# Two layers of a graph network on one core: counting the edges of each bucket in one run or in two

## The chip, the core and the metric

The kernel runs on one core of a Trainium2 chip. The metric is the device time of one launch in microseconds. Five engines work side by side, each with an instruction queue of its own: TensorE (PE), VectorE (DVE), ScalarE (ACT), GpSimd (POOL) and SyncE (SP), whose queue issues most of the DMAs. They meet through semaphores: an instruction adds to one, and a queue waits until it has reached a value.

## What is computed

1250 nodes with 512 features, 21250 edges (20000 random ones and a loop at each node), sorted by destination. A three-layer network takes at each node the mean of its neighbours' features; an edge network with a segment sum and two layer norms follow. Cut to what the change touches:

```python
deg = jax.ops.segment_sum(jnp.ones_like(dst, dtype=x.dtype), dst, num_segments=n)
inv_deg = (1.0 / jnp.clip(deg, 1.0))[:, None]
for l in range(n_layers):
    neigh = jax.ops.segment_sum(h[src], dst, num_segments=n) * inv_deg
    h = h @ Ws_self[l] + neigh @ Ws_neigh[l] + bs[l]
    if l != n_layers - 1:
        h = jax.nn.relu(h)
```

The kernel writes the segment sum as a product with the matrix A of counts: A[d, s] is the number of edges from s to d, and deg is the sum of a row.

## The kernel before

**Buckets and tiles.** The nodes are cut into NB = 10 buckets of NPB = 125 by destination. The edges lie as 125 rows of EC = 170 columns in SBUF. Each edge gets a slot, so that the edges of a bucket fill whole tiles of 128; there are TILES = 176. With this data a bucket has 17 tiles (one has 18), 171 in all, and the last five are empty.

**Phase A** (`phase_a`, up to 412.86 us in the profile) has two strands.
- *Sorting.* VectorE works out the slots (`rows_of`, L389 on: first for 34 columns, then for 136) and the tables of tiles (L407 to L417: first tile of each bucket, bucket of each tile). POOL then scatters the edges' records (8 numbers) to the table `records` in HBM by indirect DMAs, a column each: `stage` (L319) copies 17 columns and issues 17 DMAs, ten times. When all 170 have landed, SP loads the table as `recs` (L296).
- *Products.* Beside it TensorE folds weight matrices, multiplies the mesh features, and does the first layer's dense products for ten blocks of nodes (L662 on), with VectorE and ScalarE splitting numbers into a high and a low part (`w_hi`, `w_lo`; `u_hi`, `u_lo`). The products are done at 256 us.

*Counting* comes last. For each tile VectorE makes two one-hot matrices (`one_hot`, L494), from the sources (128 x 1280, L497) and from the destinations (128 x 128, L498). There are GROUP = 4 buffers, so VectorE is at most four tiles ahead. TensorE multiplies them (`count`, L684) in ten 128 x 128 matmuls (L689) that add to PSUM banks 0 to 2, and one (L692) that adds the degrees to bank 3. The banks are never cleared: after a bucket's last tile ScalarE copies them out (L575, L577) to `adj[:, c]` and `degree[:, c]`, so that each copy is a running total, and phase B takes neighbours' difference.

*Gates.* A tile must not add to a bank before the copy of the bucket before is out. TensorE's loop waits for `gate[b][u]`, counted up once a tile for each of three banks. SP opens those of even tiles, and POOL those of odd ones, both with `open_gates`:

```python
with engine.Fori(0, TILES // 2) as i:
    bucket1 = engine.value_load(k["tile_bucket1"][0:1, ds(2 * i + u, 1)], min_val=1, max_val=NB)
    for b in range(3):
        engine.wait_ge(copied_out[b], bucket1)
        engine.sem_inc(gate[b][u], 1)
```

In the trace L225 is this loop (address, counter, branch), L226 the load of a register from the table, with two register operations, and L229 the three increments.

**Phase B** (`phase_b`) begins behind a barrier of all engines. `own_counts(n)` (L848) takes the difference of two running totals on VectorE (L851). ScalarE and VectorE split it (`convert` L972, `rest` L864), TensorE sums over the neighbours (`add_up`, L1042 and L1043), and `mix` (L871) divides by the degree. At the start VectorE does own_counts(9), the degrees, own_counts(8) and `many_i` (L936), which TensorE waits for before it starts. Ten blocks follow, then the dense product of the next layer. SP loads that layer's weights to `w0` and `w1` at once. The edge network and the last layer norms come behind; they fill most of the time and aren't touched.

## Time and profile before

| | us |
|---|---|
| median of three runs | 2359.06 (2358.61 to 2361.78) |
| the profiled execution | 2361.97 |
| its span | 2360.3 |
| TensorE busy | 2217.3, 94% of the span |
| VectorE busy | 1473.0, 62% |
| ScalarE busy | 1217.3, 52% |
| GpSimd busy | 1129.5, 48% |
| mean granted clock of TensorE | 0.979 of full |

Busy time is that of compute instructions (and of POOL's making of indirect DMAs). Register, branch and semaphore instructions aren't in it, so a queue that only counts semaphores shows as idle. "idle before, releaser" says how long an engine stood still before an instruction, and what ended it. The stages that the change touches lie between 0 and 475 us.

### The profile page before, as it was taken

Reading aid. Unit: us, or ns where it says so; the run is one execution under the profiler, and the core shown is the slowest. Engines: PE = TensorE matmul, PEld = TensorE weight load, DVE = VectorE, ACT = ScalarE, POOL = GpSimd, SP = SyncE. Lnnn points to the kernel's source line nnn. Section 1 sums busy time; section 2 is a strip of 40 time slices with the busy share of each in tenths; the row PEclk is TensorE's granted clock in tenths of the full one; section 3 lists DMA queues with packets and bytes.
Section 4 is the critical chain, followed back from the end, with each engine's and each line's share of the span. In section 5 each row is a group of like instructions: output and inputs, shape, how many; then the busy total and the mean of one; then the engine's idle time right before and its main releaser. Section 6 shows DMA issues by size and latency. Waiting matters only on the chain. (4 is left out here: it accounts for less than half of the span.)

```text
span 2360.3 us, 44804 instructions
## 1 busy us (share of the span) xinstructions
PE 2217.3 (94%) x13056; PEld 1889.3 (80%) x13060; DVE 1473.0 (62%) x3261; ACT 1217.3 (52%) x2255; POOL 1129.5 (48%) x1666
## 2 busy tenths in 40 slices
PE   2999399999999999999999999999999999999798
PEld 2436298778777998989989899898988989889686
DVE  7012299534384667767676767766776677666566
ACT  0122111324234767666767677676766676667421
POOL 6777700000012556555555555565656565555323
PEclk9999699999999999999999999999999999999899
DMA  7223100101126433323333333332333333333031
GB/s 204 79 61 74 20 0 0 36 5 37 40 86 186 121 63 62 65 60 64 63 65 62 62 62 62 62 66 59 62 67 62 62 62 66 60 61 67 19 92 44
DMA packets 79034, 150.48 MB, mean 64 GB/s; under 512 B 17048, under 2 KB 18148, under 8 KB 78977
## 3 DMA queue, kind: packets, MB, share of 16 engines
q0 software_dynamic: 44864, 93.18, 20.7%
q1 hardware_dynamic: 34113, 56.57, 7.6%
q8 instruction: 33, 0.54, 0.1%
q14 instruction: 24, 0.20, 0.0%
HBM read 129.17 MB, written 20.23 MB: 63 GB/s over the span
## 5 line engine op out<-in xcount | busy, mean ns | idle before, releaser
L1453 ACT ACTIVATE b_bank<-c_bias 128x512 f32<-128x512 f32 x528 | 316.1, 599 | 15.1 <-PE b_bank L1556 5.2
L1256 POOL DMA_INDIRECT c_from_src<-s_dst_table,c_at_nodes x173 | 297.2, 1718 | 31.1 <-issue 31.1
L1633 PE MATMUL b_bank<-c_m_hi,c_pt_hi 128*128 128x512 f32 x704 | 293.2, 417 | 0.0
L1390 DVE CUSTOM_DVE_ANT_0 b_bank<-b_bank,c_p,k_floor 128x512 f32<-128x512 f32 x176 | 132.4, 752 | 255.1 <-PE b_bank L1578 254.3
L1634 PE MATMUL b_bank<-c_m_lo,c_pt_hi 128*128 128x512 f32 x704 | 276.2, 392 | 0.0
L1243 POOL DMA_INDIRECT c_from_src<-s_mesh_table,c_at_nodes x176 | 202.4, 1150 | 153.8 <-POOL c_at_nodes L1239 143.6
L1635 PE MATMUL b_bank<-c_m_hi,c_pt_lo 128*128 128x512 f32 x704 | 275.6, 391 | 0.0
L1262 POOL TENSOR_TENSOR c_dev<-c_var,k_half 128x1 f32<-128x1 f32 x176 | 99.3, 564 | 312.6 <-DVE c_var L1372 312.6
L1517 ACT ACTIVATE c_h<-c_from_src 128x512 f32<-128x512 f32 x176 | 111.3, 632 | 265.0 <-DVE c_from_src L1411 265.0
L330 POOL DMA_INDIRECT s_records<-a_stage_rec,a_stage_row x170 | 206.0, 1212 | 57.4 <-issue 53.1
L1576 PE MATMUL b_bank<-c_m_hi,c_ht_hi 128*128 128x384 f32 x704 | 223.0, 317 | 4.9 <-DVE c_ht_lo L1377 4.6
L1576 PE MATMUL b_bank<-c_m_hi,c_pt_hi 128*128 128x384 f32 x704 | 224.7, 319 | 0.0
L1578 PE MATMUL b_bank<-c_m_hi,c_ht_lo 128*128 128x384 f32 x704 | 218.8, 311 | 0.0
L1577 PE MATMUL b_bank<-c_m_lo,c_ht_hi 128*128 128x384 f32 x704 | 217.9, 309 | 0.0
L1578 PE MATMUL b_bank<-c_m_hi,c_pt_lo 128*128 128x384 f32 x704 | 217.1, 308 | 0.0
L1577 PE MATMUL b_bank<-c_m_lo,c_pt_hi 128*128 128x384 f32 x704 | 216.9, 308 | 0.0
L842 POOL TENSOR_TENSOR b_dev<-b_dev,k_half 125x1 f32<-125x1 f32 x10 | 5.9, 603 | 397.8 <-DVE b_dev L889 397.8
L1406 DVE SCALAR_TENSOR_TENSOR c_rp_lo<-c_p,c_dev,c_rp_hi 128x512 fp32r<-128x512 f32 x176 | 132.2, 751 | 78.2 <-ACT c_rp_hi L1513 74.2
L1635 PEld LDWEIGHTS b_bank<-c_m_hi,c_pt_lo 128*128 128x128 f32 x704 | 132.5, 188 | 32.0
L1513 ACT ACTIVATE c_rp_hi<-c_p,c_dev 128x512 fp32r<-128x512 f32 x176 | 127.6, 725 | 55.9 <-POOL c_dev L1278 55.8
L1449 ACT ACTIVATE c_p<-b_bank 128x512 f32<-128x512 f32 x176 | 105.7, 600 | 91.2 <-PE b_bank L1553 90.7
L689 PE MATMUL a_bank<-a_hot_dst,a_hot_src 128*128 128x128 bf16 x1760 | 111.0, 221 | 42.7 <-DVE a_hot_dst L498 37.5
(307 smaller groups left out, 5927.7 us busy)
## 6 DMA issues: line engine op xcount, KB each, us to landing
k_w<-in_L_gnn_Ws_self_dram SPq DMA_DIRECT2D x3, 1024.0 KB, 9.0
k_w<-in_L_gnn_Ws_neigh_dram SPq DMA_DIRECT2D x3, 1024.0 KB, 11.5
c_from_src<-s_mesh_table,c_at_nodes POOLq DMA_INDIRECT x176, 3.5
c_from_src<-s_dst_table,c_at_nodes POOLq DMA_INDIRECT x173, 4.8
s_records<-a_stage_rec,a_stage_row POOLq DMA_INDIRECT x170, 2.6
a_mesh<-in_L_gnn_mesh_nfeat_dram SPq DMA_DIRECT2D x10, 224.0 KB
k_h<-in_x_dram SPq DMA_DIRECT2D x1, 2240.0 KB
s_mesh_table<-a_mesh_out SPq DMA_DIRECT2D x10, 224.0 KB
```

The source lines that it names most:

```text
L330: pool.indirect_dma_start(scratch["records"], bass.IndirectOffsetOnAxis(ap=stage_row[u][:, c:c + 1], axis=0), stage_rec[u][:, c, :], None) ...
L1243: pool.indirect_dma_start(from_src[u][:], None, scratch["mesh_table"], bass.IndirectOffsetOnAxis(ap=at_nodes[u][:, 0:1], axis=0)).then_inc ...
L1256: pool.indirect_dma_start(from_src[u][:], None, scratch["dst_head" if head else "dst_table"], bass.IndirectOffsetOnAxis(ap=at_nodes[u][:, ...
L1390: dve.tensor_tensor_reduce(var1_bank[:], var1_bank[:], p[u % 2][:], 1.0 / D, k["floor"][:, 0:1], ALU.mult, ALU.add, var[u][:, 0:1]).then_i ...
L1406: dve.scalar_tensor_tensor(out=rp_lo[u][:], in0=p[u % 2][:], scalar=dev[u][:, 0:1], in1=rp_hi[u][:].bitcast(F32), op0=ALU.mult, op1=ALU.su ...
L1453: act.activation(bank[:], bias[:, m, :], ACT.Copy).then_inc(bank_set, 1)
L1576: pe.matmul(to, left[0][:, c, :], high, start=False, stop=False, skip_group_check=True)
L1577: pe.matmul(to, left[0][:, c, :], low, start=False, stop=False, skip_group_check=True)
L1578: last = pe.matmul(to, left[1][:, c, :], high, start=False, stop=(c == KC - 1), skip_group_check=True)
L1633: pe.matmul(edge_bank[:], left[0], m_hi[1][:, c, :], start=False, stop=False, skip_group_check=True)
L1634: pe.matmul(edge_bank[:], left[0], m_lo[1][:, c, :], start=False, stop=False, skip_group_check=True)
L1635: last = pe.matmul(edge_bank[:], left[1], m_hi[1][:, c, :], start=False, stop=(c == KC - 1), skip_group_check=True)
```

## The change

- The first COLS1 = 136 columns (8 of 10 stagings) are scattered to `records`, the last 34 to a second table, `records2`. VectorE works out totals at column 136 and at 170, and a second offset for the last columns. An edge's slot stays within its bucket, with the first 136 columns' edges in front.
- Tiles that the first 136 columns fill (12 or 13 a bucket, 129 in all with this data) are counted first, bucket by bucket, and the remaining 47 in a second run. So the banks are copied out EVENTS = 20 times. `order`, `place` and `event1` are built on VectorE; TensorE turns the source and destination fields by transposes and a product with `place` into the order of counting (`turn_columns`, `place_fields`), and VectorE copies them to `fields`.
- SP loads the first table as soon as 136 columns are scattered, and the second between the two halves of its gate loop. VectorE adds both at tile 100, and the fields from tile 108 on are made anew.
- POOL scatters to the end and then makes the two `w_lo` of the next layer, instead of VectorE. Its gate loop is gone; SP opens the gates of all tiles, two in an iteration.
- ScalarE writes the second run's copies to `adj_more`, partly over `w0` and `w1`, and the tenth copy a second time to `adj_mid`. Phase B adds the runs (`merge`) before it takes differences, adds two degrees, and loads the next weights only when all ten counts are done.
- The tile tables are built behind the centring of the weights, not ahead of it.

```diff
+COLS1 = 8 * SCAT
+EVENTS = 2 * NB
...
+SECOND = 25
...
-    def open_gates(engine, u):
-        engine.wait_ge(tables_ok, 1)
-        with engine.Fori(0, TILES // 2) as i:
-            bucket1 = engine.value_load(k["tile_bucket1"][0:1, ds(2 * i + u, 1)], min_val=1, max_val=NB)
-            for b in range(3):
-                engine.wait_ge(copied_out[b], bucket1)
-                engine.sem_inc(gate[b][u], 1)
+    def open_gates(engine, first, end):
+        with engine.Fori(first, end) as i:
+            for u in range(2):
+                before1 = engine.value_load(event1[0:1, ds(2 * i + u, 1)], min_val=1, max_val=EVENTS)
+                for b in range(3):
+                    engine.wait_ge(copied_out[b], before1)
+                    engine.sem_inc(gate[b][u], 1)
...
+        for u in range(2):
+            sp.wait_ge(scattered[u], 16 * COLS1 // 2)
+        sp.dma_start(recs[:], scratch["records"].rearrange("(p t) f -> p t f", p=P)).then_inc(recs_in, 16)
         sp.wait_ge(self_ok, NB)
         sp.dma_start(bias0[:], rows(t["L0_gnn_bs"][1]).broadcast_to([P, D])).then_inc(bias_next, 16)
-        for u in range(2):
-            sp.wait_ge(scattered[u], 16 * EC // 2)
-        sp.dma_start(recs[:], scratch["records"].rearrange("(p t) f -> p t f", p=P)).then_inc(recs_in, 16)
         for u in range(2):
             sp.wait_ge(job_out[u], 16 * (NJ // 2) + 16 * ((len(vectors) + 1 - u) // 2))
             sp.wait_ge(mesh_stored[u], MOVED * NB // 2)
         sp.wait_ge(bias_next, 16)
-        open_gates(sp, 0)
+        sp.wait_ge(tables_ok, 1)
+        open_gates(sp, 0, TILES // 4)
+        for u in range(2):
+            sp.wait_ge(scattered2[u], 16 * (EC - COLS1) // 2)
+        sp.dma_start(k["part2"][:], scratch["records2"].rearrange("(p t) f -> p t f", p=P)).then_inc(part2_in, 16)
+        open_gates(sp, TILES // 4, TILES // 2)
...
+        pool.memset(k["part2"][:], 0.0).then_inc(pool_const, 1)
...
-            stage(u, 0, True)
+            stage(u, 0, True, scratch["records"], scattered)
         pool.wait_ge(rows_ok, 2)
-        with pool.Fori(1, EC // (2 * SCAT)) as j:
+        with pool.Fori(1, COLS1 // (2 * SCAT)) as j:
             for u in range(2):
-                stage(u, j, False)
-        open_gates(pool, 1)
+                stage(u, j, False, scratch["records"], scattered)
+        pool.wait_ge(rows_ok, 3)
+        pool.wait_ge(pads2_out, 16)
+        for u in range(2):
+            stage(u, COLS1 // (2 * SCAT), True, scratch["records2"], scattered2)
+        for i in range(2):
+            pool.wait_ge(w_next_hi, i + 1)
+            pool.tensor_tensor(w_lo[i][:], w[i][:], w_hi[i][:].bitcast(F32), ALU.subtract).then_inc(w_next_lo, 1)
...
-        rows_of(slice(0, 2 * SCAT))
-        rows_of(slice(2 * SCAT, EC))
...
+        rows_of(slice(0, 2 * SCAT), offset)
+        rows_of(slice(2 * SCAT, COLS1), offset)
+        dve.tensor_copy(counts1[:], bank[1][:, 0:NB])
+        chain.after(dve.tensor_tensor(offset2[:], bank[0][0:EP, NB:2 * NB], totals[:, 0:NB], ALU.subtract))
+        chain.after(dve.tensor_tensor(offset2[:], offset2[:], bank[0][0:EP, 0:NB], ALU.subtract))
+        chain.after(dve.tensor_tensor(offset2[:], offset2[:], counts1[0:EP, :], ALU.add))
+        chain.after(dve.scalar_tensor_tensor(out=offset2[:], in0=starts[0:EP, :], scalar=float(P), in1=offset2[:],
+                                             op0=ALU.mult, op1=ALU.add))
+        rows_of(slice(COLS1, EC), offset2)
...
+        for c in range(EVENTS - 1):
+            dve.tensor_scalar(step_by[:], tile_no[:, 0:TILES], event_at[:, c:c + 1], jump[:, c:c + 1], ALU.is_ge, ALU.mult)
+            chain.after(dve.scalar_tensor_tensor(out=event[:], in0=tile_no[:, 0:TILES], scalar=event_at[:, c:c + 1],
+                                                 in1=event[:], op0=ALU.is_ge, op1=ALU.add))
+            chain.after(dve.tensor_tensor(order[:], order[:], step_by[:], ALU.add))
+        for c in range(2):
+            dve.tensor_scalar(place[c][:], order[:], part_no[:, c:c + 1], None, ALU.is_equal)
+        dve.tensor_copy(event1[:], event[:]).then_inc(tables_ok, 1)
...
+        dve.wait_ge(part2_in, 16)
+        dve.tensor_tensor(recs[:], recs[:], k["part2"][:], ALU.add).then_inc(recs_ok, 1)
+        for u in range(GROUP):
+            one_hot(GROUP * SECOND + u, u)
+        copy_columns(2)
+        for u in range(GROUP):
+            one_hot(GROUP * (SECOND + 1) + u, u)
+        copy_fields(2, GROUP * (SECOND + 2))
...
+        for c in range(EVENTS):
+            done = act.value_load(event_end[0:1, c:c + 1], min_val=1, max_val=TILES + 1) if c < EVENTS - 1 else TILES + 1
+            if c == NB:
+                act.wait_ge(w_next_lo, 2)
+            to = k["adj"][:, c, :] if c < NB else k[f"adj_more{c - NB}"][:]
             for b in range(3):
                 lo, hi = b * 512, min((b + 1) * 512, NB * P)
                 act.wait_ge(count_mm[b], done)
-                last = act.activation(k["adj"][:, c, lo:hi], bank[b][:, 0:hi - lo], ACT.Copy)
+                last = act.activation(to[:, lo:hi], bank[b][:, 0:hi - lo], ACT.Copy)
+                if c == NB - 1:
+                    last = act.activation(k["adj_mid"][:, lo:hi], bank[b][:, 0:hi - lo], ACT.Copy)
                 if b == 2:
-                    last = act.activation(k["degree"][:, c:c + 1], bank[3][:, 0:1], ACT.Copy)
+                    last = act.activation(k["degree_at"][:, c:c + 1], bank[3][:, 0:1], ACT.Copy)
...
+        for u in range(2 * GROUP):
+            count(GROUP * SECOND + u, u % GROUP)
+            if u == 0:
+                pe.wait_ge(recs_ok, 1)
+                turn_columns()
+            if u == GROUP + 1:
+                place_fields(2)
...
+                sp.wait_ge(counts_ok, NB)
...
+            if n:
+                merge(n - 1)
             own = k["adj"][0:NPB, n, :]
-            dve.tensor_tensor(own, own, k["adj"][0:NPB, n - 1, :], ALU.subtract).then_inc(counts_ok, 1)
+            dve.wait_ge(merged, NB - max(n - 1, 0))
+            dve.tensor_tensor(own, own, k["adj"][0:NPB, n - 1, :] if n else k["adj_mid"][0:NPB, :],
+                              ALU.subtract).then_inc(counts_ok, 1)
+        def merge(n):
+            both = k["adj"][0:NPB, n, :]
+            dve.tensor_tensor(both, both, k[f"adj_more{n}"][0:NPB, :], ALU.add).then_inc(merged, 1)
...
+        merge(NB - 1)
         own_counts(NB - 1)
-        dve.tensor_copy(degree[:, 0:1], k["degree"][:, 0:1])
-        dve.tensor_tensor(degree[:, 1:], k["degree"][:, 1:], k["degree"][:, 0:NB - 1], ALU.subtract).then_inc(degree_ok, 1)
+        dve.tensor_copy(degree_runs[:, 0:1], k["degree_at"][:, 0:1])
+        dve.tensor_tensor(degree_runs[:, 1:], k["degree_at"][:, 1:], k["degree_at"][:, 0:EVENTS - 1],
+                          ALU.subtract).then_inc(runs_ok, 1)
         dve.memset(ones[:], 1.0)
+        dve.wait_ge(runs_ok, 1)
+        dve.tensor_tensor(degree[:], degree_runs[:, 0:NB], degree_runs[:, NB:], ALU.add).then_inc(degree_ok, 1)
```

**Where instructions move.** SP's queue at the end of phase A, before: the load of the records (L296), and a loop with one register load, one tile.

```order
L290 DMA k_w<-in_L_gnn_Ws_neigh_dram 128x4x512
L292 DMA b_bias_53<-in_L_gnn_bs_dram 128x512
L296 DMA k_recs<-s_records 128x1408
L225 UNCONDITIONAL_BRANCH
L225 ISA
L226 TENSOR_LOAD k_tile_bucket
L226 ISA x2
L225 REGISTER_ALU
L225 COMPARE_AND_BRANCH
```

And now, from the same load of weights on:

```order
L315 DMA k_w<-in_L_gnn_Ws_neigh_dram 128x4x512
L318 DMA k_recs<-s_records 128x1408
L320 DMA b_bias_53<-in_L_gnn_bs_dram 128x512
L247 UNCONDITIONAL_BRANCH
L247 ISA
L249 TENSOR_LOAD a_event_106
L249 ISA x3
L249 TENSOR_LOAD a_event_106
L249 ISA x2
L247 REGISTER_ALU
L247 COMPARE_AND_BRANCH
L329 DMA a_part_62<-s_records 128x1408
```

The records' load stands ahead of bias0's; the loop has two register loads, one counter and one branch, and stands a second time behind the second table's load. POOL's queue has no such loop any more.

VectorE's queue at the start of phase B, before:

```order
L851 TENSOR_TENSOR k_adj<-k_adj 125x1280
L925 COPY b_degree<-k_degree 128x1
L926 TENSOR_TENSOR b_degree<-k_degree 128x9
L927 MEMSET b_ones 128x2
L929 TENSOR_REDUCE b_most<-b_degree 128x1
L930 TENSOR_SCALAR b_inv_degree<-b_degree 125x10
L932 TENSOR_SCALAR b_many<-b_most 128x1
L933 TENSOR_SCALAR b_many<-b_most 128x1
L851 TENSOR_TENSOR k_adj<-k_adj 125x1280
L936 CAST b_many_i<-b_bank 1x2
```

And now:

```order
L1001 TENSOR_TENSOR k_adj<-k_adj,ab_adj_more_72 125x1280
L1001 TENSOR_TENSOR k_adj<-k_adj,ab_adj_more_71 125x1280
L995 TENSOR_TENSOR k_adj<-k_adj 125x1280
L1076 COPY ab_degree_runs<-ab_degree_at 128x1
L1077 TENSOR_TENSOR ab_degree_runs<-ab_degree_at 128x19
L1079 MEMSET b_ones 128x2
L1081 TENSOR_TENSOR k_degree<-ab_degree_runs 128x10
...
L1001 TENSOR_TENSOR k_adj<-k_adj,ab_adj_more_70 125x1280
L995 TENSOR_TENSOR k_adj<-k_adj 125x1280
L1090 CAST b_many_i<-b_bank 1x2
```

Two merges (L1001) stand ahead of the first own_counts (L995), a third ahead of the second, and one addition of degrees (L1081) ahead of the maximum; all of them come before `many_i`.

## Rows read from the trace of the kernel before

**Rows 1.** Windows: stage, us, busy us of each engine (instructions), granted clock, DMA share.

```profile
256.20:294.31 38.11, 0.81 (x3) 0.32 (x4) 5.28 (x4) 3.48 (x2) 26.45 (x21) 0.53 0.14 29
294.31:412.86 118.55, 111.07 (x1936) 106.00 (x1936) 112.46 (x352) 14.26 (x40) 0.00 (x0) 0.98 0.00 0
412.86:417.93 5.07, 0.19 (x3) 0.10 (x3) 3.04 (x12) 2.20 (x3) 0.00 (x0) 0.79 0.33 93
```

**Rows 2.** Timeline, 232 to 295: start, us, engine, line, operation, idle before it.

```profile
232.10 0.21 POOL L324 COPY a_stage_row<-a_row_i 125x17 int32 x1
...
249.88 0.69 DVE L482 TENSOR_TENSOR k_h<-a_bank,b_bias 125x512 f32<-125x512 f32 x1 [4.12 <-PE a_bank L66]
...
256.20 0.35 SPq L292 DMA_DIRECT2D b_bias<-in_L_gnn_bs_dram  x1
257.91 4.67 DVE L488 TENSOR_TENSOR b_w_lo<-k_w,b_w_hi 128x2048 fp32r<-128x2048 f32 x2 [1.10 <-ACT b_w_hi L567]
...
290.21 0.34 SPq L296 DMA_DIRECT2D k_recs<-s_records  x1
294.31 0.55 DVE L497 TENSOR_SCALAR a_hot_src<-a_src_grid,k_recs 128x1280 bf16<-128x1280 int16 x1 [31.73 <-DMA k_recs<-s_records]
```

**Rows 3.** Timeline of one border between two buckets, 396.9 to 398.7.

```profile
396.94 0.17 PE L692 MATMUL a_bank<-a_ones,a_hot_dst 128*128 128x2 bf16 x1
396.97 0.72 PE L689 MATMUL a_bank<-a_hot_dst,a_hot_src 128*128 128x128 bf16 x10
...
397.39 1.36 ACT L575 ACTIVATE k_adj<-a_bank 128x512 int16<-128x512 f32 x3 [9.93 <-PE a_bank L689]
397.53 0.17 PE L692 MATMUL a_bank<-a_ones,a_hot_dst 128*128 128x2 bf16 x1
398.63 0.19 ACT L577 ACTIVATE k_degree<-a_bank 128x1 f32<-128x1 f32 x1
```

**Rows 4.** Lines L226, L225 and L229, SP's queue: duration ns, first and last start.

```profile
L226 SPq TENSOR_LOAD <-k_tile_bucket x8: 267/270/273, 308.9 to 316.7; - x8
...
L225 SPq ALU_OP  x2: 32/32/33, 295.5 to 296.6; - x2
L225 SPq FUSED_REGOPS  x2: 59/59/59, 295.8 to 296.9; - x2
...
L225 SPq MOVE  x1: 29/29/29, 290.8 to 290.8; - x1
...
L229 SPq EVENT_SEMAPHORE  x24: 17/17/17, 291.8 to 299.9; - x24
```

**Rows 5.** Waits of SP's queue, 240 to 410: for whom, us, times, longest.

```profile
SPq L229 <- ACT k_adj L575: 18.9, 18, 5.7
SPq L229 <- ACT k_degree L577: 2.8, 9, 0.3
```

**Rows 6.** Timeline of VectorE, 12 to 30.

```profile
13.56 1.74 DVE L392 SCALAR_TENSOR_TENSOR a_scan<-a_scan,a_offset,a_mask 125x34 f32<-125x34 f32 x10
23.75 0.35 DVE L407 TENSOR_SCALAR a_tile_bucket<-a_tile_no,a_starts 128x177 f32<-128x177 f32 x1
28.94 2.28 DVE L422 TENSOR_REDUCE a_mean<-a_w 128x4 f32<-128x2048 f32 x1
```

**Rows 7.** DMA issues, 255 to 262: KB, us from issue to landing.

```profile
b_bias<-in_L_gnn_bs_dram SPq DMA_DIRECT2D x1, 256.0 KB, 3.1
```

**Rows 8.** Timeline of the second phase's start.

```profile
414.83 0.82 DVE L851 TENSOR_TENSOR k_adj<-k_adj 125x1280 int16<-125x1280 int16 x1 [3.94 <-PEq L2001]
417.93 0.79 PE L1042 MATMUL b_bank<-b_u_hi,b_a_hi 125*128 125x512 f32 x1 [1.45 <-DVE b_many_i L936]
```

**Rows 9.** Timeline of the first layer's sums in steady state.

```profile
436.68 1.49 DVE L864 TENSOR_TENSOR b_a_lo<-k_adj,b_a_hi 125x1280 fp32r<-125x1280 int16 x1 [1.13 <-ACT b_a_hi L972]
```

**Rows 10.** Timeline of TensorE at the counting's start.

```profile
297.29 1.23 PE L689 MATMUL a_bank<-a_hot_dst,a_hot_src 128*128 128x128 bf16 x10
...
298.38 1.23 PE L689 MATMUL a_bank<-a_hot_dst,a_hot_src 128*128 128x128 bf16 x10
```

More of the change, by code:

```diff
@@ L154, in phase_a @@
     hot_dst = [hot(f"a_hot_dst{i}", [P, P], BF16) for i in range(GROUP)]
-    totals, offset = sb("totals", [EP, NB]), sb("offset", [EP, NB])
+    order, event, step_by = (hot(f"a_{n}", [P, TILES]) for n in ("order", "event", "step_by"))
+    place = [hot(f"a_place{i}", [P, TILES]) for i in range(2)]
+    columns_t, fields = hot("a_columns_t", [P, 4, P]), hot("a_fields", [P, 2, TILES])
+    event1 = hot("a_event1", [P, TILES], I32)
+    totals, offset, offset2 = sb("totals", [EP, 2 * NB]), sb("offset", [EP, NB]), sb("offset2", [EP, NB])
+    counts1, full, rest, full_ends, rest_ends = (
+        sb(n, [P, NB]) for n in ("counts1", "full", "rest", "full_ends", "rest_ends"))
+    full_i, event_end = sb("full_i", [P, NB], I32), sb("event_end", [P, EVENTS], I32)
+    event_at, jump = sb("event_at", [P, EVENTS]), sb("jump", [P, EVENTS])
+    part_no = sb("part_no", [P, 2])
     slot_i, slot_lo, slot_hi = (sb(n, [EP, EC], I32) for n in ("slot_i", "slot_lo", "slot_hi"))
@@ L387, in _, with rows_of @@
                                              op0=ALU.mult, op1=ALU.add))
-        def rows_of(part):
+        def rows_of(part, offset):
             for c in range(NB):
@@ L445, in _ @@
             last.then_inc(gains_ok, 1)
+        dve.wait_ge(pool_const, 7)
+        chain.after(dve.tensor_scalar(tile_bucket[:], tile_no[:], starts[:, 1:2], None, ALU.is_ge))
+        for c in range(2, NB):
+            chain.after(dve.scalar_tensor_tensor(out=tile_bucket[:], in0=tile_no[:], scalar=starts[:, c:c + 1], in1=tile_bucket[:],
+                                                 op0=ALU.is_ge, op1=ALU.add))
+        chain.after(dve.memset(tile_bucket[:, TILES:], float(NB)))
+        chain.after(dve.tensor_tensor(tile_step[:], tile_bucket[:, 1:], tile_bucket[:, :TILES], ALU.subtract))
@@ new lines, in _ @@
+        chain.after(dve.scalar_tensor_tensor(out=tile_flag[:], in0=tile_bucket[:, :TILES], scalar=1.0, in1=tile_step[:],
+                                             op0=ALU.add, op1=ALU.mult))
+        dve.tensor_copy(k["tile_last"][:], tile_flag[:])
+        dve.tensor_scalar(k["tile_bucket1"][:], tile_bucket[:, :TILES], 1.0, None, ALU.add)
+        dve.tensor_copy(k["bucket_end"][:], ends[:])
+        chain.after(dve.tensor_copy(full_i[:], counts1[:]))
+        chain.after(dve.tensor_scalar(full_i[:], full_i[:], 7, None, ALU.logical_shift_right))
@@ new lines, in _ @@
+        chain.after(dve.tensor_copy(full[:], full_i[:]))
+        chain.after(dve.tensor_tensor(rest[:], tiles_f[:], full[:], ALU.subtract))
+        dve.tensor_tensor_scan(out=full_ends[:], data0=full[:], data1=k["zeros"][:, 0:NB], initial=0.0,
+                               op0=ALU.add, op1=ALU.add)
+        chain.after(dve.tensor_tensor_scan(out=rest_ends[:], data0=rest[:], data1=k["zeros"][:, 0:NB], initial=0.0,
+                                           op0=ALU.add, op1=ALU.add))
+        dve.tensor_copy(event_at[:, 0:NB], full_ends[:])
@@ new lines, in _ @@
+        chain.after(dve.tensor_scalar(event_at[:, NB:], rest_ends[:], full_ends[:, NB - 1:NB], None, ALU.add))
+        dve.tensor_scalar(event_end[:], event_at[:], 1.0, None, ALU.add)
+        dve.tensor_copy(jump[:, 0:NB - 1], rest[:, 0:NB - 1])
+        dve.tensor_copy(jump[:, NB:EVENTS - 1], full[:, 1:NB])
+        chain.after(dve.tensor_tensor(jump[:, NB - 1:NB], full[:, 0:1], full_ends[:, NB - 1:NB], ALU.subtract))
+        chain.after(dve.tensor_tensor(jump[:, NB - 1:NB], jump[:, NB - 1:NB], rest_ends[:, NB - 2:NB - 1], ALU.subtract))
@@ new lines, in _ @@
+        dve.tensor_copy(order[:], tile_no[:, 0:TILES])
+        chain.after(dve.memset(event[:], 1.0))
+        for c in range(EVENTS - 1):
[3 more added lines that the diff above has]
+            chain.after(dve.tensor_tensor(order[:], order[:], step_by[:], ALU.add))
@@ L583, in _ @@
         pe.wait_ge(dve_const, 4)
[L584 removed]
+        pe.wait_ge(pool_const, 7)
         pe.wait_ge(totals_ok, 1)
[L586 to L587 removed]
+        pe.matmul(bank[0][0:EP, 0:2 * NB], before[0:EP, 0:EP], totals[:], start=True, stop=True)
+        pe.matmul(bank[1][:, 0:2 * NB], ones[0:EP, :], totals[:], start=True, stop=True).then_inc(totals_mm, 1)
         pe.wait_ge(centred, 3)
```

143 lines of the change are left out of this document (90 added, 53 removed).

## The prediction

> **What bounds the kernel now.** I read the windows by stage first. Between 256.20 and 294.31 us TensorE does 0.81 us of work; the counting stage runs from there to 412.86, 118.55 us; then 5.07 us pass with almost nothing on TensorE [rows 1]. TensorE is busy 94% of the whole span (the table above) and everything behind the counting is chained to it, so a microsecond gained or lost here moves the end by about as much. The timeline of the gap shows its cause: VectorE starts the first one-hot at 294.31 after 31.73 us of waiting for the records, whose load SP issued at 290.21, when the last scatter had landed [rows 2]. That gap is what the change goes for.
>
> Then the counting stage itself. VectorE is busy 112.46 of its 118.55 us with 352 operations, two for each of 176 tiles, 0.64 us a tile [rows 1]: it sets the pace. TensorE could go a little faster: the closing matmuls (L692) of two neighbouring tiles start 0.59 us apart at the full clock [rows 3]. But TensorE also waits for gates, and these are made by two instruction queues, SP for even tiles, POOL for odd ones. So I read SP's queue, which the busy shares leave out. In a stretch with nothing to wait for, eight register loads of L226 go from 308.9 to 316.7, which is 7.8/7 = 1.11 us for one gate iteration, one tile [rows 4]. 88 of them are 98 us. The waits of SP in this stage come to 18.9 + 2.8 us [rows 5]. Together 120 us, the length of the stage: SP has had only some 20% of its time to spare, with half of the tiles.
>
> **The change part by part, in the profiled execution's time (2361.97, span 2360.3; the median of the runs is 2359.06, 2.9 lower, and I carry the difference over).**
>
> Start. The tile tables (23.75 to 28.94 us on VectorE [rows 6]) move behind the centring, into time in which VectorE is idle; a third call of rows_of with ten 34-column operations (1.74 us [rows 6]) and its tail, 3.3 in all by the like steps, and four small ones on offset2 (0.9) come before it, while the middle call gets shorter by 1.0. Net 5.2 - 3.3 - 0.9 + 1.0 = 2.0; with the two added small operations I take 1.6 us earlier for TensorE's chain up to 256. Ends: 0 (the weights' load decides) and 2.0. The memset, the zero table's store, the event tables (19 rounds of three short operations, about 20 us) and columns_t lie in VectorE's and SP's idle time; I cost them at nothing. Without that cover the tables would cost those 20 us.
>
> Records. POOL stages column 136 and its sixteen followers at 232.10, so the first 136 have landed near 235; the load takes 294.31 - 290.21 = 4.1 us, so 239. The product loop's last step asks for it after the ninth step's matmuls, near 249 [rows 2]: ten us of slack. The first one-hot could start near 257. **But the gates can't open then**: SP loads bias0 at 256.20 as before, it lands in 3.1 us [rows 2, 7], and SP enters its loop at 259.3 - 1.6 = 257.7.
>
> Gates. This is the term that decides. POOL's loop is gone, since POOL scatters; SP now runs all 176 tiles, two in an iteration. What the pair saves is one add, one branch and the jump: from ALU_OP at 296.6 to the next FUSED_REGOPS at 296.9 [rows 4], which I take as 0.24. So a pair costs 2 x 1.115 - 0.24 = 1.99 us, 1.0 a tile, against 0.64 that VectorE needs. 88 pairs: 175.1, plus 0.3 for entering (MOVE at 290.8 to the first gate at 291.8 [rows 4]). **SP becomes the pace.** VectorE's additions in the stage (the sum of both tables about 1.7 us, copies of columns and fields about 1.2) hide in the 0.36 us a tile that it now waits; TensorE's eight transposes and four-matmul groups do too.
>
> Events. Banks are copied out 20 times instead of 10, with 19 borders to pass instead of 9. At a border SP now stands in the wait itself. From the rows of one border [rows 3]: the bucket's last tile starts at 396.97, ScalarE at 397.39, 0.42 later; degree's copy ends at 398.63 + 0.19 = 398.82, 1.43 after ScalarE's start. The third gate of the next tile then opens 0.42 + 1.43 + 0.1 - 0.09 = 1.86 us after the third gate of the last one, against 1.0 without a border: 0.86 each, 19 x 0.86 = 16.3. The tenth copy is made twice (adj_mid), 1.4 more. SP's load of the second table between its two loops costs 0.7; it is issued near 350, 60 us after the scatter's end, and has some 8 us until VectorE, at most four tiles ahead, needs it: 4.1 are enough.
>
> End of counting: 257.7 + 175.1 + 0.3 + 16.3 + 1.4 + 0.7 = 451.5 for the last gate, and 0.42 + 1.43 - 0.09 to the last copy, 453.3. Before it is 412.86: **40.4 us later**.
>
> w_lo. Two operations of 4.67 us together [rows 2] go from VectorE to POOL behind the scatter, at 290; ScalarE asks for them at the eleventh copy, near 400. Hidden, and would be at ten times the price.
>
> Second phase. Ahead of the first sum VectorE has three merges more, each like L851's 0.82, and a degree addition with its wait. Two merges stand before own_counts(9), one before own_counts(8), all in front of many_i, for which TensorE waits before it starts at 417.93 [rows 8]: 3 x 0.82 + 0.3 = 2.8 us. The merges inside the loop lie in a wait: the L864 in the steady state had waited 1.13 us for ScalarE [rows 9], a merge takes 0.82. The weights' load now waits for the tenth count, still a whole layer ahead of its use. Ends: 0.8 (one merge) and 5.
>
> Sum: 40.4 + 2.8 = 43.2. **2359.06 + 43.2 = 2402 us**, 1.8% slower; the profile would say 2405. A measurement of this kernel tells 0.2%, 4.7 us, from no change.
>
> Bounds. For a gated tile, 0.875 (the loop's 0.24 saved on each) and 1.115 (on none) are the ends: 154 and 196 us, a total of 2381 to 2423. I take 1.0, since the loads, register operations and six semaphore steps are the same and only their loop end is shared. For a border the ends are 0.6, if half of the copies ran beside the next load, and 1.4, the whole copy: 2397 to 2412.
>
> **A rule weighed.** Tiles at 297.29 and 298.38 show the low level of the clock: 1.09 us a tile against 0.59 at the full one [rows 3, 10]; they follow the long gap, whose granted clock is 0.53 [rows 1]. With gates at 1.0 us TensorE works 0.6 of the time. If it fell to the low level there, 1.09 would replace 1.0. The Trainium skill (TensorE: Matmul & The Clock Gate, Part 1) says that the low level comes after an idle window and names a kernel whose short pauses between groups of matmuls made the clock swing between 1.2 and 2.4 GHz. By its first statement nothing is added to my sum; by the second up to the price of rival 2. No stretch of this trace has such a rhythm.
>
> **Rivals.**
> 1. *SP keeps up, faster.* If a tile's gates in the longer body cost under 0.64, VectorE stays the pace. Then counting starts at 256.2 instead of 294.31 and takes 118.55 + 2.9 for VectorE's additions, 10 x 0.6 for borders (VectorE's idle 6.1 us in the stage lie at nine borders and the cold start [rows 1]), 1.4 for adj_mid: 385.1, 27.8 earlier, less 2.8 behind: 2334 us. For it: the gap in [rows 1] is real and all of the other terms are small. Against it: [rows 4]; the body would have to run 1.8 times as fast. The deciding point is 1.0 - 43.2/176 = 0.75 us a tile: below it the new kernel wins. Chance 8%.
> 2. *The low clock holds in the gated stage.* A tile takes 1.09, 176 x 0.09 = 16 more at most, and a border's 0.42 grows to some 0.7, 5 more; a fully busy TensorE regains the clock, so about half of that: 2412. Chance 12%.
> 3. *The gate loop binds only in part*, because SP's lead or the borders hide one another: 10 us less, 2392. This lies in the forecast's own range; chance 10%. That the change doesn't do what it says would show as a records wait of VectorE before its first one-hot; the ten us of slack in [rows 2] speak against it, and I give it nothing of its own.
>
> **How the numbers follow.** Forecast 68%, rival 3 10%, rival 2 12%, rival 1 8%, within 0.2% 2% (several errors of one sign). Range: 2387 to 2420, which leaves out rival 1 and the corners of both bounds. Faster 0.08, same 0.02, slower 0.90.
>
> **What the profile would show.** Right: the gap at 256 gone, the first one-hot near 257, the first count near 259; VectorE's L-lines of one_hot waiting for TensorE in nearly every tile; TensorE waiting for SPq some hundred times; SP's register loads 0.9 and 1.1 apart by turns; counting about 194 us long; own counts near 455. Wrong: SP with long waits for ScalarE and loads faster than 0.75 apart, or counting ended before 400.

## The result, and the profile after

The change takes 2412.74 us (median of four runs, 2408.44 to 2413.62) beside 2360.42 for the kernel before on the same chip: a ratio of 1.0222 [1.021, 1.0235], 2.2% slower. Of the four executions of the kernel before that stand beside it one took 3005.05 us; the other three have the median 2359.06, and the change is 53.7 above it. I had forecast 2402, slower, within 2387 to 2420. The profiled execution took 2408.44 us (span 2406.7), where I had expected the profile to say 2405.

Windows of the changed kernel, as in [rows 1]: the start, the counting before, in and behind a stall, and the start of the second phase.

```profile
256.40:260.90 4.50, 1.86 (x9) 0.92 (x9) 4.01 (x10) 3.50 (x2) 3.82 (x5) 1.00 0.22 62
260.90:287.40 26.50, 19.66 (x275) 17.00 (x275) 21.50 (x45) 1.43 (x4) 21.91 (x17) 0.94 0.08 3
287.40:296.20 8.80, 2.19 (x20) 1.89 (x21) 8.80 (x9) 1.43 (x4) 6.42 (x2) 0.56 0.00 0
296.20:461.00 164.80, 117.27 (x1656) 96.63 (x1653) 105.88 (x298) 25.87 (x72) 0.00 (x0) 0.98 0.01 5
461.00:466.50 5.50, 0.00 (x0) 0.00 (x0) 3.09 (x12) 1.78 (x5) 0.00 (x0) 0.63 0.00 0
```

The 38 us gap is gone, and the counting behind it fills 201 us in place of 118.55. In the last long window neither engine is full: TensorE 117 and VectorE 106 of 164.80 us, where VectorE had 112.46 of 118.55 [rows 1]. Something that is in no column sets the pace. The waits between 255 and 460 us name it (for whom, us, times, longest):

```profile
DVE a_hot_src L584 <- PE a_bank L820: 54.0, 123, 2.0
PE a_bank L817 <- SPq L252: 52.2, 156, 2.5
...
PE a_bank L817 <- DVE a_hot_dst L585: 9.9, 5, 7.5
```

VectorE waits for TensorE, and TensorE 156 times for an increment of SP's queue (L252, the gates). SP's own waits for the copies (230 to 470) are short but for one of 7.6 us, which is the stall below; so its queue is busy and not held up:

```profile
SPq L252 <- ACT k_adj L676: 12.9, 14, 7.6
SPq L252 <- ACT ab_degree_at L680: 6.1, 19, 0.6
SPq L252 <- ACT ab_adj_more L676: 5.8, 14, 0.6
```

The register loads of the gate loop, from 262 to 270 us (duration ns, first and last start), correspond to [rows 4]:

```profile
L249 SPq TENSOR_LOAD <-a_event x8: 262/270/315, 262.3 to 269.1; - x8
```

Eight loads are 6.8 us apart, 0.97 a tile; followed one by one they stand 0.9 and 1.1 us apart by turns, up to the last at 459.5.

The timeline holds one thing that I had not foreseen. When the last scatter's issue ends, near 285, GpSimd does the two w_lo, and VectorE stands inside a single one-hot until both are done (start, us, as in [rows 2]):

```profile
283.54 0.23 DVE L585 TENSOR_SCALAR a_hot_dst<-a_dst_grid,a_fields 128x128 bf16<-128x128 int16 x1
...
284.16 9.72 DVE L585 TENSOR_SCALAR a_hot_dst<-a_dst_grid,a_fields 128x128 bf16<-128x128 int16 x1
...
284.85 8.96 POOL L382 TENSOR_TENSOR b_w_lo<-k_w,b_w_hi 128x2048 fp32r<-128x2048 f32 x2
...
293.93 1.25 PE L817 MATMUL a_bank<-a_hot_dst,a_hot_src 128*128 128x128 bf16 x10 [7.46 <-DVE a_hot_dst L585]
...
294.58 1.36 ACT L676 ACTIVATE k_adj<-a_bank 128x512 int16<-128x512 f32 x3 [19.80 <-PE a_bank L817]
```

The same operation takes 0.23 us a moment earlier. The one that stands has the earlier start of the two, 284.16 against 284.85. The last counting, the merges and the first sum correspond to [rows 8]:

```profile
461.86 0.19 ACT L680 ACTIVATE ab_degree_at<-a_bank 128x1 f32<-128x1 f32 x1
463.32 1.56 DVE L1001 TENSOR_TENSOR k_adj<-k_adj,ab_adj_more 125x1280 int16<-125x1280 int16 x2 [5.47 <-PEq L2155]
...
469.08 0.78 PE L1196 MATMUL b_bank<-b_u_hi,b_a_hi 125*128 125x512 f32 x1 [2.31 <-DVE b_many_i L1090]
```

The last copy ends at 462.05 against 412.86, 49.2 later (forecast 40.4); the first sum starts 51.15 later than at 417.93.

### The profile page after: what moved, and what is told of

The parts are those of the page before. It is cut to its first block and busy times, and to the rows that moved or that the text cites. A ratio compares the mean times of both kernels' runs of the same rounds, so it can differ in the third digit from the quotient of the medians.

```text
span 2406.7 us, 44790 instructions
## 1 busy us (share of the span) xinstructions
PE 2244.7 (93%) x13080; PEld 1897.9 (79%) x13084; DVE 1537.0 (64%) x3375; ACT 1234.0 (51%) x2298; POOL 1123.4 (47%) x1669
## 5 line engine op out<-in xcount | busy, mean ns | idle before, releaser
L1397 POOL DMA_INDIRECT c_from_src<-s_mesh_table,c_at_nodes x176 | 196.8, 1118 | 154.0 <-POOL c_at_nodes L1393 144.7
L817 PE MATMUL a_bank<-a_hot_dst,a_hot_src 128*128 128x128 bf16 x1760 | 136.3, 224 | 63.4 <-SPq L252 52.4
L817 PEld LDWEIGHTS a_bank<-a_hot_dst,a_hot_src 128*128 128x128 bf16 x1760 | 104.0, 100 | 86.7 <-SPq L252 41.4
```

What stands on the lines that cost most here:

```text
L817: last = pe.matmul(bank[b][:, (s % 4) * P:(s % 4 + 1) * P], hot_src[u][:, s * P:(s + 1) * P], hot_dst[u][:], start=False, stop=False, skip ...
L1397: pool.indirect_dma_start(from_src[u][:], None, scratch["mesh_table"], bass.IndirectOffsetOnAxis(ap=at_nodes[u][:, 0:1], axis=0)).then_inc ...
```

## The experiments

Theory A: SP's queue, with a register load and three waits a tile, is the pace. Theory B: VectorE and GpSimd shut each other out while GpSimd does w_lo. The rivals: the twenty copies and VectorE's additions make the loss; the low clock does; the stall is a wait for something else.

All results in one table; the last copy's start and the first sum are read in the timeline of each profiled execution, the median stands beside a kernel before at 2359.1 to 2360.4.

| kernel | last degree copy | first sum | median us | ratio to before |
|---|---|---|---|---|
| before | 412.67 | 417.93 | 2359.06 | 1 |
| the change | 461.86 | 469.08 | 2412.74 | 1.0222 [1.021, 1.0235] |
| e0_again | 458.34 | 465.58 | 2410.09 | 1.0219 [1.0201, 1.0236] |
| e1_wlo_vector | 456.10 | 463.33 | 2406.34 | 1.0196 [1.0179, 1.0213] |
| e2_two_queues | 412.36 | 420.66 | 2368.93 | 1.0038 [1.0026, 1.0051] |
| e3_before_sp | 471.77 | 476.28 | 2418.42 | 1.0248 [1.023, 1.0265] |
| e4_runs | 405.93 | 413.16 | 2354.21 | 0.9979 [0.9969, 0.9988] |
| e5_runs_vector | 398.81 | 406.04 | 2348.16 | 0.9952 [0.9935, 0.9969] |
| e6_runs_late_bias | 398.78 | 406.01 | 2350.34 | 0.9956 [0.994, 0.9973] |
| e7_two_queues_vector | 409.19 | 417.52 | 2362.23 | 1.0015 [1.0005, 1.0024] |
| e8_before_runs | 407.32 | 411.82 | 2355.72 | 0.998 [0.997, 0.9989] |
| e9_wlo_twice | 415.45 | 422.68 | 2363.42 | 1.0021 [1.0011, 1.003] |
| e10_wlo_pieces | 409.81 | 417.04 | 2353.40 | 0.9974 [0.9963, 0.9985] |
| e11_best_again | 399.75 | 406.98 | 2346.28 | 0.9946 [0.9933, 0.996] |

### The change once more, and w_lo back on VectorE

e0_again is the change, unedited. Expected:

> The changed kernel once more, beside the same runs of before as the next three. Every theory: 2.1 to 2.3% slower, 2408 to 2414 us, counting ended (last copy out of PSUM) near 462 us. The profiled execution of the change was 2408.4 and the three others 2412 to 2414; the theory that this spread is TensorE's clock in the last phase expects that the granted clock behind 2280 us goes with it, and that the stages up to there agree within 1 us.

The median is within the expected range. But this second profiled execution ends its counting 3.5 us earlier than the first, and not within 1 us of it. The expectation on the clock holds: behind the first sum it takes 1941.5 us, with a granted clock of 0.88 over its last 156 us, where the first took 1937.6 with 0.92. In its timeline the stall is there, but TensorE waits at another place:

```profile
285.07 10.11 DVE L584 TENSOR_SCALAR a_hot_src<-a_src_grid,a_fields 128x1280 bf16<-128x1280 int16 x1
...
295.40 1.25 PE L817 MATMUL a_bank<-a_hot_dst,a_hot_src 128*128 128x128 bf16 x10 [7.00 <-DVE a_hot_dst L585]
```

SP goes on opening gates while VectorE stands, until the next border between buckets. In the first execution that border came in the middle of the stall, and two neighbouring loads there were 9.11 us apart in place of 1.64: 7.5 lost. Here it came later, 5.66 in place of 1.64: 4.0 lost.

e1_wlo_vector:

```diff
-        for i in range(2):
-            pool.wait_ge(w_next_hi, i + 1)
-            pool.tensor_tensor(w_lo[i][:], w[i][:], w_hi[i][:].bitcast(F32), ALU.subtract).then_inc(w_next_lo, 1)
...
         copy_fields(1, 0)
+        for i in range(2):
+            dve.wait_ge(w_next_hi, i + 1)
+            dve.tensor_tensor(w_lo[i][:], w[i][:], w_hi[i][:].bitcast(F32), ALU.subtract).then_inc(w_next_lo, 1)
```

> The two w_lo go back from GpSimd to VectorE, ahead of the first one-hot, and nothing else. Theory 'VectorE and GpSimd shut each other out': in the profile of the change one L585 takes 9.72 us while GpSimd makes the w_lo (8.96 us from 284.85), TensorE waits 7.46 us; this goes, and the 4.7 us on VectorE at 258 hide in the 0.36 us that it waits per tile: 8 to 9 us less than e0. Rival 'the stall is a late gate or record, and w_lo only stands beside it': the stall stays, 0 to 3 us more than e0.

Measured 3.75 us less than e0_again, under half of what I expected. No operation of VectorE near 285 is longer than 3 us any more, and TensorE's waits for VectorE are 7.8 us, the longest (5.0) at the start. I had priced the whole stall; but SP's pace hides the part of it up to the next border, and 4.0 is what e0_again had left to win. SP's loads at both borders stand 1.64 apart here, and from its first load to its last it takes 192.8 us in place of 196.5.

### Two queues for the gates

e2_two_queues keeps everything of the change, and lets GpSimd open the odd tiles' gates once SP has opened the first 36 tiles:

```diff
-        open_gates(sp, 0, TILES // 4)
+        open_gates(sp, 0, 18)
+        sp.sem_inc(handed, 1)
+        open_half(sp, 0, 18, TILES // 4)
...
+        pool.wait_ge(handed, 1)
+        open_half(pool, 1, 18, TILES // 2)
```

> SP opens all gates of the first 36 tiles, and from there on SP those of even and GpSimd those of odd tiles, as before the change; w_lo stays on GpSimd. Theory 'SP's gate loop is the pace': up to tile 36 as in e0 (near 306 us), then 140 tiles at 0.64 plus 17 borders at 0.65, the tenth copy 1.4 and VectorE's additions 3: last copy near 412 instead of 462, the kernel at 2360 to 2364, no change against before. Rival 'the twenty copies, the merging of tables and the longer queue of VectorE are the price': less than 10 us better than e0.

46 us of counting come back, with all twenty copies, VectorE's additions and GpSimd's w_lo still in place: those rivals are out as the main cause. The last copy is where it was expected; the median is 5 us above the range that I gave and 9 above before's, while the profiled execution was the fastest of the six. TensorE's waits from 255 to 470 us:

```profile
DVE a_hot_src L596 <- PE a_bank L832: 17.1, 31, 1.6
PE a_bank L829 <- SPq L252: 9.0, 23, 2.5
PE a_bank L829 <- DVE a_hot_dst L597: 8.2, 3, 7.0
```

e3_before_sp puts the suspected cost alone into the kernel before: no second run, no additions, only SP for all gates.

```diff
         with engine.Fori(0, TILES // 2) as i:
+            for u in range(2):
...
-        open_gates(pool, 1)
```

> The kernel before, with its gates opened by SP alone, two tiles in an iteration; nothing else of the change. Theory 'SP's gate loop is the pace': 88 pairs at 1.99 us and 9 borders at 0.86 from 290.8 on, the last copy at 476 instead of 413 us, 63 us slower than before (2.6%). Rival 'two queues' worth of work fits in one, since the waits are shared': slower by less than 10 us.

The last copy comes 59.1 us later and the kernel is 58.5 slower (63 expected). Its first one-hot came 3.0 us earlier than in the profile of before, so the stage itself grew by 62.1 us. Its waits in the same stretch, and eight register loads from 300 to 308 us:

```profile
DVE a_hot_src L497 <- PE a_bank L692: 51.3, 156, 0.8
PE a_bank L689 <- SPq L230: 45.3, 155, 0.7
```

```profile
L227 SPq TENSOR_LOAD <-k_tile_bucket x8: 262/264/273, 300.2 to 308.0; - x8
```

It is the pattern of the change, in a kernel that has nothing else of it. Theory A is shown from both sides, and for most of the loss: e1_wlo_vector, the change without the stall, is still 46.5 us slower than before.

### A cheaper loop on one queue

e4_runs asks whether SP as such is slow, or only this loop. The copies are waited for once a run of tiles, and the loop over its tiles only counts up; TensorE waits for one gate a bank (`gate[b][0]`, n + 1).

```diff
-        with engine.Fori(first, end) as i:
-            for u in range(2):
-                before1 = engine.value_load(event1[0:1, ds(2 * i + u, 1)], min_val=1, max_val=EVENTS)
+        for c in range(first, end):
+            at = engine.value_load(event_end[0:1, c - 1:c], min_val=1, max_val=TILES) if c else 1
+            stop = engine.value_load(event_end[0:1, c:c + 1], min_val=1, max_val=TILES + 1) if c < EVENTS - 1 else TILES + 1
+            for b in range(3):
+                engine.wait_ge(copied_out[b], c + 1)
+                engine.sem_inc(gate[b][0], 1)
+            with engine.Fori(at + 1, stop):
                 for b in range(3):
-                    engine.wait_ge(copied_out[b], before1)
-                    engine.sem_inc(gate[b][u], 1)
+                    engine.sem_inc(gate[b][0], 1)
```

> The change with another gate loop, still SP alone: each of the 20 runs of tiles between two copies waits for the copies once, and the loop over its tiles holds only three increments, no register load of a table and no wait. Counts on TensorE, copies, borders and w_lo on GpSimd are those of the change. Theory A (SP's loop with its load, waits and increments is the pace at 1.0 us a tile): SP now takes under 0.5 us a tile, VectorE at 0.64 is the pace again; stage 112.6 for 176 tiles, 19 borders x 0.65, 1.4 for adj_mid, 3.3 for the additions of VectorE, and now the whole 8.8 us in which VectorE and GpSimd shut each other out: last degree copy near 398.5, against 458 to 462 in the change; kernel near 2347, faster than before. TensorE's waits for SP under 15 us in place of 52. Rival B (the loss is in the twenty copies and VectorE's additional work, SP only looks late): over 2385.

56 us less than e0_again, and 0.2% faster than before: the change wins, by a little, once its gates are cheap. TensorE's waits for SP fell from 52.2 to 9.6 us. SP's increments there, in e5_runs_vector (same loop), from 392.5 to 396.5:

```profile
L255 SPq EVENT_SEMAPHORE  x16: 17/17/17, 392.6 to 395.8; - x16
```

Two of a tile's three increments stand on this line, so these are eight tiles; followed one by one, a tile takes 0.44 us, against 1.0. But the last copy came at 405.9 where I expected 398.5. TensorE's timeline in the second run of e5_runs_vector, where a bucket has four or five tiles, shows why:

```profile
384.37 1.03 PE L820 MATMUL a_bank<-a_hot_dst,a_hot_src 128*128 128x128 bf16 x10 [0.47 <-SPq L252]
...
388.05 1.03 PE L820 MATMUL a_bank<-a_hot_dst,a_hot_src 128*128 128x128 bf16 x10 [0.47 <-SPq L252]
...
391.72 1.02 PE L820 MATMUL a_bank<-a_hot_dst,a_hot_src 128*128 128x128 bf16 x10 [0.47 <-SPq L252]
```

Four tiles take 3.67 us: 4 x 0.585 on TensorE and 1.33 for the border (3.42 in other buckets of four). Here VectorE (4 x 0.64 = 2.56) waits; TensorE and the copies are the pace. My prices, VectorE's 0.64 a tile and 0.65 a border, give 3.21. In e4_runs the ten buckets of the second run, from the tenth degree copy (366.43) to the last (405.93), take 39.5 us where these prices give 47 x 0.64 + 10 x 0.65 = 36.6. That is 2.9 of the missing 7.4. The rest lies earlier: TensorE's first count came at 261.52 where my sum leaves 260.0 for it, and the first run took 3.0 more.

e5_runs_vector is e4_runs with the edit of e1_wlo_vector, and e6_runs_late_bias moves SP's wait for bias0 behind the loops as well:

```diff
-        sp.wait_ge(bias_next, 16)
...
         open_runs(sp, 6, EVENTS)
+        sp.wait_ge(bias_next, 16)
```

> e4_runs with w_lo on VectorE ahead of the one-hots, as in the kernel before. Theory A with the exclusion of VectorE and GpSimd: in this kernel nothing covers the stall near 285, so taking it away gains its whole 8.8 us, less the 4.7 us of VectorE's own work on w_lo, part of which lies in waiting for the gates at the start: 4 to 6 us less than e4_runs, near 2342, last degree copy near 394; no matmul waits over 3 us for VectorE behind the start. Rival (the stall near 285 is a wait for something else, that w_lo does not cause): 0 to 5 us more than e4_runs.

> e5_runs_vector, with SP's wait for the landing of bias0 (2.7 us in the change) moved behind both gate loops. If the gates set when counting starts: 2 us less than e5_runs_vector. If VectorE's w_lo, which ends near 262, sets it: 0 to 0.5 us less. I hold the second for likelier, since w_lo lies ahead of the first one-hot.

e5 is 6.05 us under e4, about as expected (its absolute figures, near 2342 and 394, are off by nearly what e4's were); where SP is not the pace nothing hides the stall. e6 changes nothing that its four executions can show (2344.72 to 2350.43, those of e5 2346.0 to 2350.6; the last copy 398.78 against 398.81): the first one-hot stands behind VectorE's w_lo in both, at 262.65 and 262.29.

e7_two_queues_vector is e2_two_queues with the same edit:

> e2_two_queues (SP opens the first 36 tiles alone, then SP the even and GpSimd the odd ones) with w_lo on VectorE ahead of the one-hots. In e2_two_queues VectorE is the pace once two queues open the gates; the w_lo on GpSimd holds it for about 9 us, but also holds GpSimd's first gates. Without it, and with 4.7 us on VectorE at the start, which SP's pace of 1.0 us a tile hides: 4 to 8 us less than e2_two_queues, 2361 to 2365, last degree copy 404 to 408. If SP's first 36 tiles hide the stall as well: no difference.

Measured 2362.23, 6.7 under e2_two_queues; by the first sums of the two profiled executions 3.1. The last copy came at 409.2, one later than the range I gave.

### What the stall is

e9_wlo_twice repeats each w_lo on GpSimd (two instructions of 4.5 us more), e10_wlo_pieces cuts each in 16; both are e4_runs otherwise.

```diff
+            pool.tensor_tensor(w_lo[i][:], w[i][:], w_hi[i][:].bitcast(F32), ALU.subtract).then_inc(once, 1)
+            pool.wait_ge(once, i + 1)
             pool.tensor_tensor(w_lo[i][:], w[i][:], w_hi[i][:].bitcast(F32), ALU.subtract).then_inc(w_next_lo, 1)
```

> e4_runs with each of the two w_lo subtractions on GpSimd done twice, the second time with the same result. If VectorE and GpSimd shut each other out while GpSimd runs them: VectorE stands still for 18 us in place of 9, and since SP is not the pace here nothing hides it: 9 us more than e4_runs, 2363. If the 9.7 us of VectorE near 285 come from something that happens once (a first use, a load): no change.

9.2 us more than e4_runs, where 9 were expected. Its timeline:

```profile
283.17 5.17 DVE L590 TENSOR_SCALAR a_hot_dst<-a_dst_grid,a_fields 128x128 bf16<-128x128 int16 x1
283.78 4.50 POOL L385 TENSOR_TENSOR b_w_lo<-k_w,b_w_hi 128x2048 fp32r<-128x2048 f32 x1
288.26 0.54 DVE L589 TENSOR_SCALAR a_hot_src<-a_src_grid,a_fields 128x1280 bf16<-128x1280 int16 x1
288.36 4.80 POOL L387 TENSOR_TENSOR b_w_lo<-k_w,b_w_hi 128x2048 fp32r<-128x2048 f32 x1
288.72 4.48 DVE L590 TENSOR_SCALAR a_hot_dst<-a_dst_grid,a_fields 128x128 bf16<-128x128 int16 x1
293.12 4.49 POOL L385 TENSOR_TENSOR b_w_lo<-k_w,b_w_hi 128x2048 fp32r<-128x2048 f32 x1
293.13 4.83 DVE L589 TENSOR_SCALAR a_hot_src<-a_src_grid,a_fields 128x1280 bf16<-128x1280 int16 x1
297.69 4.62 POOL L387 TENSOR_TENSOR b_w_lo<-k_w,b_w_hi 128x2048 fp32r<-128x2048 f32 x1
297.88 4.48 DVE L590 TENSOR_SCALAR a_hot_dst<-a_dst_grid,a_fields 128x128 bf16<-128x128 int16 x1
```

Each GpSimd instruction holds one of VectorE's to its end, four times 4.5 to 5.2 us. The Trainium skill (SBUF — State Buffer, "SBUF: two separate sides") calls the SBUF port pair that both share an exclusive lock and not a split: of a GpSimd operation and a VectorE operation in a two-port mode, or with two inputs in SBUF beside a GpSimd operation that reads SBUF, the one that starts first holds it for its whole instruction and the other blocks. The rows agree in that VectorE stands still and doesn't merely slow down, and e9 shows the price. They don't settle who comes first: the first of the four held one-hots has the earlier start (283.17 against 283.78), as in the change, though GpSimd was then still making its last indirect DMA; the other three start behind GpSimd's instruction. No row tells in which mode a one-hot runs.

> e4_runs with each w_lo subtraction on GpSimd cut into 16 of 128 columns. Tells whether small pieces let VectorE in between. If GpSimd holds VectorE only while an instruction of its own runs, and VectorE gets its turn between two: GpSimd's 32 pieces are spread, VectorE's loss is still their sum, 9 us and more with 32 starts, but never in one piece, so nothing is gained: 2354 to 2358. If the loss is one of turns only (whoever comes first runs to its end): part of it falls into VectorE's waits at the borders and the total is 2 to 4 us under e4_runs.

The pieces did not let VectorE in (from 283 us on):

```profile
283.52 13.91 DVE L592 TENSOR_SCALAR a_hot_dst<-a_dst_grid,a_fields 128x128 bf16<-128x128 int16 x1
283.88 13.88 DVE L591 TENSOR_SCALAR a_hot_src<-a_src_grid,a_fields 128x1280 bf16<-128x1280 int16 x1
284.13 13.25 POOL L388 TENSOR_TENSOR b_w_lo<-k_w,b_w_hi 128x128 fp32r<-128x128 f32 x32
```

32 pieces take 13.25 us in a row, and VectorE got no turn between any two of them. In e9 it ended an operation at each of the three borders between GpSimd's four. At two of them GpSimd waited for its own result. At the third, near 293.1, stands only the wait for w_next_hi, long satisfied, which stands between the two w_lo of the change and e4_runs too, and there VectorE got no turn. The first sum came 3.9 us later than in e4_runs; the profiled execution was the slowest of its eight, and the medians (2353.40, from executions of 2348.83 to 2361.28, and 2354.21) do not tell the two apart. What decides the turn stays open.

### How much is the loop, how much the second run

e8_before_runs gives the kernel before the loop of e4_runs (with `bucket_end` in place of `event_end`) and takes GpSimd's away; e11_best_again is e5_runs_vector once more, beside it.

> The kernel before with the gate loop of e4_runs: SP alone opens all gates, the waits for the copies once a bucket, three increments a tile, GpSimd's loop gone. Tells how much of the gain of e5_runs_vector is in the loop and how much in counting in two runs. Theory (before, the two loops with a register load each are hidden: TensorE's waits for both queues are 3.9 us in the stage): a bucket of 17.6 tiles takes 17.6 x 0.64 = 11.3 on VectorE, or 17.6 x 0.59 + 1.33 = 11.7 on TensorE with its border; the stage is 118.55 now, so 0 to 3 us less: 2356 to 2359. Rival (the loop is all of the gain): about 2348, like e5_runs_vector.

> e5_runs_vector once more, with more rounds, beside e8_before_runs on the same chip: 2348, 11 us under the kernel before, and last degree copy near 399.

The loop alone is worth 3.4 us to the kernel before (0 to 3 expected), e11 is 12.8 under before (11 expected), and their intervals do not meet. So counting in two runs does gain something of its own: 9.4 us by the medians, of which the first sums of the two profiled executions show 4.8. The rest lies behind the first sum, where nearly the same work takes 1943.8 us in e8's profile and 1937.6 in e11's (below); no run shows that the way of counting causes that. The profile of e8 holds one more thing that the edit doesn't explain: GpSimd's last scatter issue ends at 286.05 in place of 288.74 in before, so that the first one-hot comes 2.8 us earlier; the stage itself takes 115.96 us in place of 118.55. In e3_before_sp it ends at 285.62. Why was not tried. The fastest version is e5_runs_vector: two medians, 2348.16 and 2346.28.

## Why the prediction was right, and where it was not

- **SP becomes the pace.** Right, with its size: 1.99 us a pair was forecast, 0.87 and 1.11 by turns measured. e2 and e3 show that it makes nearly all of the loss, and e1 that 46.5 us of it are there without the stall.
- **Borders.** 0.86 each was forecast. SP's loads at the borders stand 2.0 to 2.1 apart (once 2.4) in place of 1.1, and 1.6 in place of 0.9; over the nineteen the mean is 0.88 more, without the stall and without the tenth copy's second writing, which costs 1.25 (1.4 forecast). Right.
- **w_lo "hidden, and would be at ten times the price".** This step failed. I looked at when its result is needed (near 400) and not at what it does to its neighbour while it runs. It cost 7.5 us in the profiled execution and 4.0 in e0_again. The trace of before had the hint: a copy of `stage` that takes 0.21 us at 232.10 [rows 2] took 1.77 beside VectorE's w_lo (from 257.91 on), and I had not looked at it:

```profile
258.67 1.77 POOL L324 COPY a_stage_row<-a_row_i 125x17 int32 x1
```

- **Start, 1.6 us earlier.** VectorE's chain was 1.5 ahead at 37 us, but at 249 the difference was 0.2, and bias0's issue came at 256.42 against 256.20. In the other kernels with this start it lies between 255.89 and 257.59, in the two others with the old start at 256.39 and 257.49. The gain is within what executions differ by; my lower end, 0, was right. SP's first load came at 259.9, 2.2 later than forecast.
- **The sum of the stage.** From SP's first load to the last copy I had 453.3 - 257.7 = 195.6, measured 462.05 - 259.9 = 202.15: 6.55 more, which is the stall (7.5) less about 1.
- **Second phase.** 2.8 forecast; from the last copy to the first sum it takes 7.03 in place of 5.07, 2.0 more. The merges inside the loop are hidden as expected.
- **VectorE as the old pace.** This reading was wrong, though the forecast doesn't rest on it. I took it from VectorE's busy time (0.64 a tile). The waits inside the old stage (296 to 412.8) say that TensorE with its borders was the pace, by a little: it waited 0.3 us for VectorE, and VectorE 3.2 for it. Between borders its closing matmuls stand about 0.585 apart. The 0.64 came back in rival 1 and in what I expected of e4_runs.

```profile
DVE a_hot_src L497 <- PE a_bank L692: 3.2, 12, 0.4
PE a_bank L689 <- DVE a_hot_dst L498: 0.3, 1, 0.3
```

- **Rival 2, the low clock.** Out. In the gated stage the granted clock is 0.98, the level of 2.4 GHz nearly throughout, with TensorE busy 117 of 165 us. It fell in the stall, where TensorE did nothing for 7.46 us: 0.56 in that window. Of the two statements of the Trainium skill that I had weighed (TensorE: Matmul & The Clock Gate, Part 1) the first, that the low level comes after an idle window, fits the stall; the second, a clock that swings with short pauses, did not come true here, where pauses of 0.33 us in nearly every tile (52.2 us in 156) did not bring the clock down.
- **Rival 1, SP keeps up.** Out as the kernel stands. Its deciding point, 0.75 us a tile, is bracketed and not measured: at 1.0 the kernel loses, at 0.44 (e4) it wins by 0.2%, and with two queues (e2) the counting ends with the old one. Its price of 2334 was too good: with cheap gates and w_lo on VectorE (e5) the last copy comes at 398.8 and not at 385.1.
- **The total.** 51.15 at the first sum became 46.4 at the end of the profiled executions. The last 156 us went at a granted clock of 0.92, against 0.88 before:

```profile
2250.70:2406.70 156.00, 127.58 (x624) 105.08 (x622) 96.86 (x187) 38.56 (x61) 45.46 (x60) 0.92 0.19 54
```

```profile
2204.30:2360.30 156.00, 127.16 (x601) 104.28 (x599) 94.29 (x182) 35.87 (x57) 44.52 (x56) 0.88 0.19 54
```

From the first sum to the end it is 1937.6 us in the changed kernel's profiled execution and in e11's, but 1941.5 to 1942.9 in those of before, e0, e1 and e5. So the medians (52 to 54 us apart) say more of the change than the two profiles (46), and the forecast's miss is 10.7 us against the first median, 8 against e0_again's. The quick last phase goes with the higher clock there; which of them brings the other, and why only some executions have it, stays open.

## What to carry to other kernels

A queue that only loads registers and counts semaphores shows as idle in every busy share; when work on it is doubled, read its period from the starts of one of its own instructions, and put it beside the tile's. If it is too slow, take the load and the waits out of the inner loop before taking a second queue: wait once a run and let the loop only increment. And before an elementwise operation goes from VectorE to an idle GpSimd, ask what VectorE does meanwhile: here the two subtractions took 9 us on GpSimd and stopped VectorE for 9 us, where on VectorE itself they take 4.5 us together.

## What the runs showed of the hardware

- GpSimd's subtraction of 128 x 2048 floats (4.5 us) holds a VectorE one-hot of 0.24 us to its end; two of them in a row made one last 9.72 us. On VectorE both together take 4.5 us, so moving them doubled what VectorE pays.
- Thirty-two small instructions in a row shut VectorE out longer (13.9 us) than two large ones (9.72). Where GpSimd waited for its own result between two instructions (e9) VectorE had a turn, and once where it did not.
- GpSimd is slower beside VectorE's w_lo too. In e5_runs_vector its making of an indirect DMA, 1.19 us as a rule, takes 3.31; in e11_best_again, the same kernel, two such take 1.89 and 1.90:

```profile
256.36 1.19 POOL L364 DMA_INDIRECT s_records<-a_stage_rec,a_stage_row  x1 [0.30 <-issue]
...
258.23 4.49 DVE L578 TENSOR_TENSOR b_w_lo<-k_w,b_w_hi 128x2048 fp32r<-128x2048 f32 x2 [0.19 <-ACT b_w_hi L668]
258.29 3.31 POOL L364 DMA_INDIRECT s_records<-a_stage_rec,a_stage_row  x1 [0.30 <-POOL a_stage_rec L359]
```

- An iteration of SP's loop with one table load, three waits and three increments takes 1.11 us (before), one with two of each 1.98 (the change), one with three increments alone 0.44 (e5_runs_vector).
